# Retention: a block's scores move directly behind its projection of q and k, the output projection behind that of v, and the masking ahead of the rotation

## The reference, cut to what matters

```python
normed = (x - mu) * lax.rsqrt(var + EPS) * ln_w + ln_b
q, k = rope(normed @ Wq) * dk ** (-0.5), rope(normed @ Wk)     # 4 heads of 64
v, g = normed @ Wv, normed @ Wg                                # 4 heads of 128
def step(S, inp):                                              # one chunk of tokens
    attn = jnp.einsum('bhid,bhjd->bhij', qn, kn) * Dmask
    o = attn @ vn + (qn * cross) @ S
    S = S * gC + jnp.einsum('bhid,bhiv->bhdv', kn * kdec, vn)
o = o * lax.rsqrt((o ** 2).mean(-1) + EPS) * g_norm_w
out = x + (o * silu(g)) @ Wo
```

## Time and profile before

| what | value |
|---|---|
| median of 3 runs | 2998.61 us (2994.41 to 2998.64) |
| the profiled execution | 2997.11 us |
| its span, first to last instruction | 2995.5 us |
| busy share of the span | PE 95%, PEld 49%, DVE 68%, ACT 58%, POOL 42% |
| retention of sequence 3 | about 1135 to 1222 us |
| passes 3 to 6 of it | 11.4 us each |
| granted TensorE clock in them | 1.00 |

### The profile page before, as it was taken

How to read it: one execution, slowest core, us unless ns; L and a number is a source line. 1 busy time by engine, 2 the same in 40 slices (tenths; PEclk the granted TensorE clock), 3 DMA queues, 4 the chain that set the end, 5 groups by cost and what they waited for, 6 DMA issues and landing times.

```text
span 2995.5 us, 51610 instructions
## 1 busy us (share of the span) xinstructions
PE 2846.0 (95%) x18786; PEld 1468.0 (49%) x18786; DVE 2046.4 (68%) x4319; ACT 1730.9 (58%) x3667; POOL 1250.3 (42%) x1764
## 2 busy tenths in 40 slices
PE   5989999999999999999999999999999999999997
PEld 3643356533564336643466434664346543465334
DVE  4469835797358964589545895469944699447992
ACT  2428844388344883448734586446864378543784
POOL 2315533355333553335533355334543345433453
PEclk8979999999999999999999999999999999999999
DMA  6032000510006000050001500024000230003300
GB/s 182 1 87 41 2 1 1 123 31 4 1 1 141 16 2 1 12 130 16 2 1 26 116 16 2 1 44 98 16 1 1 65 78 16 1 1 85 58 2 15
DMA packets 54781, 107.59 MB, mean 36 GB/s; under 512 B 12401, under 2 KB 34977, under 8 KB 54401
## 3 DMA queue, kind: packets, MB, share of 16 engines
q1 hardware_dynamic: 54400, 104.26, 14.9%
q10 hardware_dynamic: 128, 0.03, 0.0%
HBM read 56.66 MB, written 36.72 MB: 31 GB/s over the span
## 4 chain that ended last, share of the span: by engine, by line
PE 77%; DVE 12%; POOL 4%; issue 3%; SPq 2%; ACT 2%; DMA 2%; POOLq 0%; DVEq 0%; ACTq 0%
PE psum L785 19%; PE psum L841 16%; PE psum L574 11%; DVE mx L1511 6%; PE psum L894 4%; PE psum L612 3%; PE psum L816 3%; PE psum L751 3%; PE psum L634 2%; PE psum L948 2%; PE psum L875 2%; PE psum L932 2%; PE psum L951 2%; POOL X L1620 1%; PE psum L650 1%
## 5 line engine op out<-in xcount | busy, mean ns | idle before, releaser
L1511 DVE TENSOR_REDUCE mx<-psum 128x1 f32<-128x512 f32 x2048 | 1266.1, 685 | 88.1 <-PE psum L785 87.6
L1255 ACT ACTIVATE Z<-psum 128x512 f32<-128x512 f32 x2048 | 1109.7, 598 | 280.3 <-PE psum L816 252.4
L1710 POOL TENSOR_TENSOR Z<-Z,band_exp 128x256 f32<-128x256 f32 (+1 forms) x1152 | 711.7, 640 | 688.9 <-ACT Z L1255 681.4
L785 PE MATMUL psum<-SK,SQ 63*128 63x512 f32 x2048 | 800.5, 470 | 29.5 <-DVE mx L1511 23.0
L816 PE MATMUL psum<-SQ,SK 64*128 64x512 f32 x2048 | 758.9, 472 | 8.9 <-DMA SQ<-mrow 8.4
L841 PE MATMUL psum<-Z,Vx 128*17 128x256 f32 x8192 | 642.3, 388 | 0.4 <-POOL Z L1710 0.4
L785 PEld LDWEIGHTS psum<-SK,SQ 63*128 63x128 f32 x2048 | 329.7, 191 | 482.0 <-DVE mx L1511 363.6
L574 PE MATMUL psum<-Wqkvg,Z 128*128 128x512 f32 x768 | 367.6, 605 | 1.0 <-ACT Z L1148 1.0
L816 PEld LDWEIGHTS psum<-SQ,SK 64*128 64x128 f32 x2048 | 311.4, 189 | 80.5 <-ACT Z L1255 37.0
L841 PEld LDWEIGHTS psum<-Z,Vx 128*17 128x17 f32 x8192 | 138.3, 95 | 334.5 <-issue 274.1
L1655 POOL TENSOR_TENSOR Z<-Z 128x512 f32<-128x512 f32 x64 | 81.1, 1268 | 299.5 <-DVE Z L1434 299.5
(11 more groups left out here) (125 smaller groups left out, 3264.2 us busy)
## 6 DMA issues: line engine op xcount, KB each, us to landing
parts<-Z SPq DMA_DIRECT2D x32, 512.0 KB
X<-L_attn_a_x SPq DMA_DIRECT2D x8, 1024.0 KB, 5.5
SQ<-parts SPq DMA_DIRECT2D x32, 256.0 KB, 7.8
SK<-parts SPq DMA_DIRECT2D x32, 256.0 KB, 10.7
SQ<-parts SPq DMA_DIRECT2D x16, 512.0 KB, 6.5
SK<-parts SPq DMA_DIRECT2D x16, 512.0 KB, 14.2
out<-X SPq DMA_DIRECT2D x16, 512.0 KB, 18.8
SQ<-mixed SPq DMA_DIRECT2D x96, 64.0 KB, 2.5
```

The costliest lines, as they stand in the source:

```text
L785: pe.matmul(row_bank(c), SQ[rows_of(h, MAX_ROW), h // 2, i * P:i * P + P], SK[rows_of(h, MAX_ROW), h // 2, 512 * k:512 * k + 512], start=T ...
L1255: nc.scalar.activation(ring[:, n % RING, :], col_bank(n), ACT.Exp)\
L1511: nc.vector.tensor_reduce(mx2[:, blk % 2, col, k:k + 1], row_bank(2 * u + k), AX_X, ALU.max)\
L1710: nc.gpsimd.tensor_tensor(ring[:, n % RING, a:z], ring[:, n % RING, a:z], band_exp[:, 4 * hg + cols_of(s)[i], at:at + z - a], ALU.mult)\
```

## The change

It gives the same instructions another order on two engines. TensorE: `y_project(t - 3)` no longer stands between `qk_of(t)` and the scores of t - 1 but behind the projection of v, directly ahead of the output of t - 1. VectorE: the mask of t - 1 stands directly behind the norm of z, ahead of the rotation of t and of `x_out(t - 3)`. No instruction is added or removed, and no transfer is touched.

```diff
--- before.py
+++ after.py
@@ -920,8 +920,6 @@
                         ln_transposes(b, 0)
                     if 1 < t < NT:
                         qk_of(b, t)
-                    if 3 <= t <= NT:
-                        y_project(b, t - 3)
                     if 1 <= t <= NT:
                         u = t - 1
                         need(pe, kq_T, b, 3 * u + 3)
@@ -938,6 +936,8 @@
                     if 0 < t < NT:
                         need(pe, v_cp, b, t)
                         project(b, t, 1, 512, p_v)
+                    if 3 <= t <= NT:
+                        y_project(b, t - 3)
                     if 1 <= t <= NT:
                         need(pe, att_m, b, u + 1)
                         need(pe, v_cp, b, u + 1)
@@ -1420,6 +1420,12 @@
                 for t in range(NT + 1):
                     if t + 1 < NT:
                         z_norms(b, t + 1)
+                    if 1 <= t:
+                        u = t - 1
+                        need(dve, att, b, u + 1)
+                        need(dve, p_o, b, u)
+                        nc.vector.tensor_tensor(AT[:, :], bank[4], mask[:, :], ALU.mult)\
+                            .then_inc(att_m.sem, 1)
                     if t < NT:
                         need(dve, p_qk, b, t + 1)
                         need(dve, rope_qk, b, t)
@@ -1436,11 +1442,6 @@
                     if t >= 3:
                         x_out(b, t - 3)
                     if 1 <= t <= NT:
-                        u = t - 1
-                        need(dve, att, b, u + 1)
-                        need(dve, p_o, b, u)
-                        nc.vector.tensor_tensor(AT[:, :], bank[4], mask[:, :], ALU.mult)\
-                            .then_inc(att_m.sem, 1)
                         if t == NT:
                             mixes(b, 0, (0,))
                         if u < NT - 1:
```

## The result

The changed kernel takes 2985.0 us (median of 6 runs, 2979.1 to 2987.6), the kernel before 2996.0 beside it (6 runs, 2994.4 to 2998.6). The ratio is 0.9961, 95% interval 0.9948 to 0.9973: faster by 11 us, 0.4%. The span of the profiled execution went from 2995.5 to 2984.0, by 11.5 us.

What follows compares the result with a forecast made beforehand. The prediction took TensorE to bound the kernel (77% of the chain), with avoidable waits in pass 8. Gain 8 x 1.54 = 12.3 us, no cost elsewhere, took 2998.6 to 2986 us; range 2982 to 2992, wider 2980 to 2992.5.

Steps and rivals of the forecast that it cites:

- Where the gain is: Pass 8: scores go first and the output projection fills TensorE's wait for the mask; other passes cost 0.
- Its size: Pass 8, layernorm's transposes to first output pair: 1.54 us gained per sequence, bounds 1.01 to 1.78.
- the bound of 1.78 with a hidden load: Pass 8: if the scores' weight load is hidden, they take 0.86 us and the gain is 1.78 per sequence.
- Passes 3 to 7 at no cost: TensorE's sum of groups stays unchanged, 11.41 us a pass; VectorE's rotation is 1.47 us late, slack 2.4, cost 0.
- Where TensorE waits: Two places per sequence: pass 1 before the first scores, for ScalarE's kT copy (untouched), and pass 8.
- Pass 1 at no cost, thinly: Pass 1: rotation 3.70 us late, GpSimd's product ends 1147.53, transposes' load about 1147.7; cost 0, upper bound 0.3 us.
- rotation becomes the bound: Pass 1, L975's wait on GpSimd's product: if none of 3.70 us is covered, 3016 us, slower; chance 0.05.
- Given back at the channel mix: At L612: if `mixes` releases it, only 0.75 us per sequence is gained, 2992.6 us; margin 0.4; chance 0.08.
- More is gained: Passes from 3 on: if the output projection load's 0.45 us wait for yT lengthened them, 18 us more, 2968; chance 0.04.
- The sum and the level: Whole kernel: 8 x 1.54 = 12.3 us off the median 2998.6, giving 2986 us, -0.4%; chance 0.77.

Runs made afterwards that it cites:

- the spare operation: The changed kernel plus one unused 128x4 power operation on GpSimd in pass 1, ahead of its product: 2992.1 us, ratio 0.9982.
- the mask-first kernel with v(1) ahead: The changed kernel with v(1) projected ahead of the scores of block 0 in pass 1, mask still ahead of the rotation: 2985.0 us, ratio 0.9960.
- its twin: The changed kernel with v(1) ahead of the scores in pass 1, but the rotation ahead of the mask there: 2979.0 us, ratio 0.9939.

## Why the prediction was right, point by point

- **Where the gain is.** Stated: pass 8 alone. The two kernels with the edits in pass 8 only and everywhere but there gave 2982.9 and 2996.5. Shown.
- **Its size.** Stated 1.54 us per sequence. From the first copy of S to the first low part of q, a stretch that holds passes 2 to 8 and the channel mix, the eight sequences gained 1.53, 1.54, 1.54, 1.54, 1.54, 1.56, 1.55 and 1.52, together 12.32. In sequence 3 the terms are these: before, 0.46 of wait for yT, 0.77 for the mask, and 0.26 and 0.27 for the two groups that started from a standstill; after, one toll of 0.25 on the scores, 1.11 against 0.86. The scores' 1.13 from a standstill was 1.11, so the bound of 1.78 with a hidden load was not reached; the load waited 0.21 us for its semaphore, with the transposes still running. TensorE didn't stand still here; the toll fell due because the load started only at 1210.59, when the transposes ended.
- **Passes 3 to 7 at no cost.** Held: 11.41 us. The kernel with the edits everywhere but in pass 8 takes in pass 2 as well.
- **Where TensorE waits.** The prediction named two places of a sequence. The chain has one more in retention, in pass 0, where the transposes (L975, 1139.53 in sequence 3) wait for GpSimd's product (L1662, in the chain from 1138.46 for 1.02 us); the change doesn't touch it.
- **Pass 1 at no cost, thinly.** Held. The cover of 0.19 us was measured by the spare operation; the prediction had read 1147.88 against about 1147.7. That the two agree so closely is partly luck. Its figure for the product's end was 0.35 us ahead of the group's turn (1147.53 and 1147.88), and it measured 0.43, since the rotation began at 1138.09, before the end of the mask's row at 1138.17. Against 0.43 the edge lies 0.24 us ahead of the turn, not 0.18. The load L975 moved by 0.21 us, not by 0.3: it stood 0.59 ahead of the turn (1147.29) and now stands 0.38 ahead (1142.40). The root behind the product ends at 1142.71 + 1.02 = 1143.73, and y starts at 1144.12, 1.34 us behind the group's turn as before (1149.22 and 1147.88), so that was covered too. The rival "rotation becomes the bound" has the right place, but the change stops 0.19 us short of it; the mask-first kernel with v(1) ahead went past, and is 6 us slower than its twin.
- **Given back at the channel mix.** The margin was read as 0.4; `mixes` ends at 1213.83 + 1.41 = 1215.24 and L612 starts at 1215.67, 0.43. Nothing was given back. The price of this rival was summed a little high: 1221.10 less 1220.41 is 0.69 us, not 0.75, which makes 5.5 us of the 6.
- **More is gained.** The first load of the output projection waited for yT in passes 3 to 7, by 0.45 us. In its new place it waits for nothing but the issue, 0.24 us, and these passes are as long as before: that wait had cost TensorE nothing.
- **The sum and the level.** 12.3 forecast, 11.5 in the span and 11.0 between the medians. Retention and channel mix gave 12.32; 0.32 came ahead of sequence 0's first mark; seven attentions together took 1.1 more. Two executions of one code differ in them by 4.8, so the missing 0.8 isn't a cost of the change as far as one can tell. The length of the stretches at the lower clock goes with the difference, as shown above; no run set it, so it stays a correlation, and it doesn't say why a stretch is short or long. The 2986.3 rested on 2998.6, the median of three runs; six runs of the kernel before gave 2996.0, and from there the same sum would have given 2983.7, against 2985.0 measured. So the forecast of 2986 holds a level that was 2.6 us too high and a gain that was 1.3 us too large, and the two errors partly cancel. The size of the gain is the test that it passed; how close the level came is luck.

## What to carry to other kernels

Read the chain for the places where a saturated engine stands still, and count the whole toll of one: the wait, and the slower start of the next group, about 0.26 us here for each. In a pipeline written out by hand the first and the last pass lack the filler of the middle ones, so an order tuned for the middle costs there, and an order by pass (`if t == 1`, `if t == NT`) is free. Before moving work between two engines' queues ask what stands behind it on the second: TensorE's half of this change alone lost 55 us, since the mask was queued behind an addition that waited for the moved product.

## What was unexpected of the hardware

A weight load that waits 0.45 us for its input cost TensorE nothing. The input was there 0.43 us before the group's turn in the chain (1142.35 and 1142.78), and the load still ran beside the matmuls in flight. The distance to the edge was 0.19 us, if past it each bit of lateness passes through in full, so for this group the edge lies about 0.24 us ahead of its turn, an estimate from the kernel with the spare operation. The kernel with v(1) first and the mask first bears that out: it brought the first copy of S 0.7 us forward and lost 0.7 again before pass 8 (72.9 us from mark to mark became 73.6). Another group has another toll: the scores of pass 8, whose load started 0.02 us ahead of their turn, paid 0.25.
